# A three-layer perceiver block for 16 pairs of batches: every engine's order of work written anew

## The chip, the cores and the metric

The kernel runs on one core of a Trainium2 chip, in one launch. The metric is the device time of that core in microseconds, a median over runs. Five engines have programs of their own and meet only at semaphores: TensorE (PE, matmuls and transposes), VectorE (DVE), ScalarE (ACT), GpSimd (POOL) and SyncE (SP, which here only issues DMAs).

## The reference

Input are x, 32 batches of 64 rows of 512, and a context of 128 rows of 512 for each batch, all in float32. Three residual layers follow, each on the layer-normalised x:

```python
# 1: cross attention, 16 heads, low-rank
C_q, C_kv = norm(x) @ Wq_d, ctx @ Wkv_d                 # 512 -> 64, 512 -> 32
scores = einsum((C_q @ W_qk) per head, C_kv) / sqrt(32)   # 16 x (64 x 128) a batch
x = x + softmax(scores) @ (C_kv @ Wv_u)
# 2: self attention over the 64 rows, one head of width 128
q, k, v = norm(x) @ Wqkv + bqkv
x = x + softmax(q k^T / sqrt(128)) v @ Wo + bo
# 3: quantised layer
xh = norm(x) @ hadamard                                   # 512 x 512
xq = clip(round(xh / s), -8, 7) * s,  s = max|xh| / 7 of the row
x = x + xq @ ternary(weight)^T
```

## The kernel before

The 32 batches are worked as 16 pairs; a pair's 2 x 64 rows fill the 128 partitions. A pair goes through a chain of small steps, each a matmul group into one PSUM bank and a read of it by ScalarE or VectorE:

- latents: the columns of x and of the context (tiles xt, ct) give the latents (L633, L645; copy to lat), these give q_t (L669) and, spread by a matmul with a folded identity, ckv (L683).
- cross attention: scores of 16 heads into four banks (L612), maxima of eight heads at a time (L435) and their scaling by the row's layer-norm factor (L439), sixteen exponentials on ScalarE (L310 and L313; those of L310 sum their rows too, those of L313 leave the sum to VectorE, L532), a 32 by 32 transpose of the probabilities on VectorE (L445), the weighted sum of the latents into the same four banks (L716, copy u_t), its expansion (L730, tile xo in PSUM), the division by the row sums and the residual (L451, L457: x2).
- self attention: statistics on VectorE (L464), the normalised x2n on GpSimd (L262), its transpose (L638), q, k and v (L655, 24 matmuls into one bank), scores (L678), maximum, exponential (L361), transpose of p (L697), product with v (L706, o2t), output (L722), residual (L556: x3), transpose of x3 (L737).
- quantised layer: the Hadamard product (L622, the costliest group), the row's largest magnitude (L492), rounding by adding a large constant (L340, L508), transpose (L661), the ternary product in bf16 (L691, L701), scaling (L549), residual on GpSimd (L294) and the store.

The order of each engine is written out by hand in a function `body(i, ...)`, one for each engine. Round i holds, on every engine, the latents of pair i+1, the cross attention of pair i, the self attention of pair i-1 and the quantised layer of pair i-2. An engine takes its instructions strictly in that order; what it waits for are the counters `made`, `read` and `done`, through `after`. Rounds -1 to 3 and 12 to 17 are written out, rounds 4 to 11 are a hardware loop of two rounds a turn:

```python
with eng.Fori(*LOOP) as j:
    body(j * 2, j, 0, True, True, True, True)
    body(j * 2 + 1, j, 1, True, True, True, True)
```

PSUM has eight banks: 0 to 3 hold the scores and then the weighted sums, so scores(i+1) wait for the copy of u of pair i. The four others (B1 to B4) are shared: B1 by q, k, v and ckv and xo, B2 by the transposes and q_t, B3 by the latents and the small products of the self attention, B4 by the quantised layer. One-off work lies in the first rounds: the centred query weights, the constant row of the biases, the ternary weights (VectorE, L412 to L427, then transposed by L597), the Hadamard matrix less its row mean (GpSimd, L283 to L289).

## Time and profile before

| | |
|---|---|
| median of 3 runs | 357.31 us (356.91 to 358.39) |
| the profiled execution: its time, its span | 358.43 us, 356.6 us |
| TensorE busy | 308.3 us, 86% of the span, 4612 matmuls |
| VectorE busy | 251.1 us, 70% |
| ScalarE busy | 191.7 us, 54% |
| GpSimd busy | 93.1 us, 26% |
| chain that ended last | PE 35%, DVE 25%, ACT 24%, issue 11% |
| read from memory, written | 20.71 MB, 4.19 MB |

The span is the time from the first to the last instruction. A busy share is the mean over stages that are not alike, and the ends of matmuls are modelled: whether TensorE is at its limit in a stage is read from the starts of its groups. A chain's shares tell who held the end back, each for a part of the time.

### The profile page before, as it was taken

How to read it: one execution, taken by the hardware profiler on the slowest of the kernel's cores; microseconds unless marked ns; L12 is line 12 of the kernel's file. 1: busy time of each engine (PE TensorE's matmuls, PEld its weight loads, DVE VectorE, ACT ScalarE, POOL GpSimd, SP SyncE). 2: the span in 40 equal slices, each digit the busy share in tenths (PEclk: the TensorE clock that was granted, in tenths of full speed). 3: DMA queues.
4: the chain of work that ended last, by engine and by line, in shares of the span. 5: the costliest groups of instructions: out<-in, count | busy, mean ns of one | idle time of the engine just before them, and what ended most of it. 6: DMA issues, size and time to landing. Idle time of an engine off the chain costs nothing.

```text
span 356.6 us, 11424 instructions
## 1 busy us (share of the span) xinstructions
PE 308.3 (86%) x4612; PEld 203.9 (57%) x4612; DVE 251.1 (70%) x530; ACT 191.7 (54%) x629; POOL 93.1 (26%) x133
## 2 busy tenths in 40 slices
PE   5766759999798999899999999999999999968871
PEld 3445447665456566666666565657575666645520
DVE  1454883878587787778787878788787878767432
ACT  1360652847547483829384756657484839282210
POOL 2004232323212221314132323222222223131321
PEclk9995687999999999999999999999999999998997
DMA  7980210303113130303040312213132020000000
GB/s 219 332 304 2 67 54 8 113 4 93 56 35 119 33 118 31 118 29 118 3 141 3 102 45 51 96 29 118 31 119 63 2 61 2 33 2 31 0 31 29
DMA packets 13345, 25.37 MB, mean 71 GB/s; under 512 B 3200, under 2 KB 3712, under 8 KB 13312
## 3 DMA queue, kind: packets, MB, share of 16 engines
q1 hardware_dynamic: 13312, 24.91, 21.5%
q8 instruction: 23, 0.38, 0.4%
q14 instruction: 10, 0.08, 0.1%
HBM read 20.71 MB, written 4.19 MB: 70 GB/s over the span
## 4 chain that ended last, share of the span: by engine, by line
PE 35%; DVE 25%; ACT 24%; issue 11%; POOL 2%; DMA 1%; POOLq 0%; DVEq 0%; ACTq 0%
ACT prob L313 11%; DVE mx L435 10%; PE ps L716 9%; PE ps L612 6%; PE ps L722 5%; PE ps L730 4%; DVE nmx L439 3%; ACT prob L310 3%; PE ps L737 3%; DVE stat L464 3%; DVE stat L483 3%; PE ps L706 2%; POOL rstd L267 2%; ACT q_t L301 2%; ACT p2t L301 2%
## 5 line engine op out<-in xcount | busy, mean ns | idle before, releaser
L310 ACT ACTIVATE prob<-ps,nmx,qk_scale 128x128 f32<-128x128 f32 x128 | 56.7, 457 | 39.5 <-DVE nmx L439 39.5
L622 PE MATMUL ps<-had_s,x3t 128*128 128x512 f32 x128 | 59.2, 606 | 1.4 <-ACT x3t L301 1.4
L313 ACT ACTIVATE prob<-ps,nmx,qk_scale 128x128 f32<-128x128 f32 x128 | 48.5, 489 | 0.0
L435 DVE TENSOR_REDUCE mx<-ps 128x8 f32<-128x1024 f32 x32 | 39.0, 1220 | 10.0 <-PE ps L612 10.0
L445 DVE STREAM_TRANSPOSE prob_t<-prob 128x1024 f32<-128x1024 f32 x32 | 39.1, 1223 | 6.9 <-ACT prob L313 6.9
L294 POOL TENSOR_TENSOR res<-prod,x 128x512 f32<-128x512 f32 x16 | 20.2, 1264 | 82.0 <-DVE prod L549 82.0
L622 PEld LDWEIGHTS ps<-had_s,x3t 128*128 128x128 f32 x128 | 23.0, 190 | 27.2 <-issue 25.3
L655 PEld LDWEIGHTS ps<-x2t,wqkv_s 128*128 128x128 f32 x256 | 30.9, 198 | 10.4 <-ACT x2t L301 10.4
L716 PE MATMUL ps<-prob_t,ckv_n 32*32 32x128 f32 x2048 | 33.1, 300 | 4.0 <-DVE prob_t L445 2.5
L655 PE MATMUL ps<-x2t,wqkv_s 128*128 128x128 f32 x256 | 33.9, 288 | 2.9 <-ACT x2t L301 1.4
L259 POOL TENSOR_TENSOR rstd<-aux,power 128x1 f32<-128x1 f32 x16 | 8.8, 548 | 91.5 <-DVE aux L470 91.5
L716 PEld LDWEIGHTS ps<-prob_t,ckv_n 32*32 32x32 f32 x2048 | 26.2, 108 | 8.4 <-issue 4.9
L556 DVE SCALAR_TENSOR_TENSOR x<-ps,rsum,x2b 128x512 f32<-128x512 f32 x16 | 12.0, 751 | 26.7 <-PE ps L722 26.7
L301 ACT ACTIVATE x3t<-ps 128x512 f32<-128x512 f32 x16 | 9.6, 597 | 33.9 <-PE ps L737 33.9
L310 ACT ACTIVATION_READ_ACCUMULATOR prob<-ps,nmx,qk_scale 128x1 f32 x128 | 26.1, 204 | 0.0
L301 ACT ACTIVATE u_t<-ps 128x512 f32<-128x512 f32 x16 | 9.6, 597 | 30.6 <-PE ps L716 30.6
L279 POOL TENSOR_TENSOR qk_scale<-aux,power 128x1 f32<-128x1 f32 x16 | 8.8, 548 | 61.5 <-DVE aux L518 61.5
L669 PE MATMUL ps<-lat,wqk 128*128 128x128 f32 x128 | 19.7, 302 | 4.3 <-ACT lat L301 4.3
L730 PEld LDWEIGHTS ps<-wv_bd,u_t 128*128 128x128 f32 x128 | 17.0, 201 | 9.2 <-issue 8.7
L612 PE MATMUL ps<-ckv,q_t 32*64 32x128 f32 x1024 | 20.9, 296 | 0.6 <-ACT ckv L301 0.6
L669 PEld LDWEIGHTS ps<-lat,wqk 128*128 128x128 f32 x128 | 17.2, 209 | 6.0 <-ACT lat L301 6.0
L276 POOL TENSOR_TENSOR x2b<-x,const_row 128x512 f32<-128x512 f32 x16 | 20.4, 1274 | 0.0
(112 smaller groups left out, 559.7 us busy)
## 6 DMA issues: line engine op xcount, KB each, us to landing
ct<-ctx_cols SPq DMA_DIRECT2D x16, 512.0 KB, 4.0
xt<-x_cols SPq DMA_DIRECT2D x16, 256.0 KB, 2.7
xr<-x_rows SPq DMA_DIRECT2D x16, 256.0 KB, 2.7
y<-res SPq DMA_DIRECT2D x16, 256.0 KB, 3.6
w_rows<-weight SPq DMA_DIRECT2D x1, 1024.0 KB, 7.9
had_s<-hadamard SPq DMA_DIRECT2D x1, 1024.0 KB, 7.0
wqkv_s<-wqkv SPq DMA_DIRECT2D x1, 768.0 KB, 8.3
wqk<-w_qk SPq DMA_DIRECT2D x2, 128.0 KB, 4.5
```

What stands on the lines that cost most here:

```text
L276: nc.gpsimd.tensor_tensor(x2b[:], x2[:], const_row[:], ALU.add).then_inc(done["x2b"], 1)
L301: return nc.scalar.activation(dst, src, ACT.Copy)
L310: last = nc.scalar.activation(prob[:, h, :], score, ACT.Exp, bias=nmx[:, h:h + 1], scale=scale, accum_out=sum_a[:, h:h + 1])
L313: last = nc.scalar.activation(prob[:, h, :], score, ACT.Exp, bias=nmx[:, h:h + 1], scale=scale)
L435: V.tensor_reduce(mx[:, h], ps[:, 2 * half:2 * half + 2, :].rearrange("p r (c k) -> p (r c) k", c=EC), AX.X, ALU.max).then_inc(done["mx"], 1)
L445: return V.transpose(prob_t[:, 2 * half:2 * half + 2, :, :, :].rearrange("p r c b q -> p (r c b q)"), prob[:, 8 * half:8 * half + 8, :].re ...
L612: mm = pe.matmul(ps[64 * bb:64 * bb + 64, r, c * P:(c + 1) * P], q_t[g, bb, c, :], ckv[g, par, bb * SKV:(bb + 1) * SKV], start=True, stop= ...
L622: mm = pe.matmul(ps[:, B4, :], x3t[:, c, :], had_s[:, c, :], start=(c == 0), stop=(c == EC - 1))
L655: mm = pe.matmul(ps[:, B1, s * P:(s + 1) * P], w if s < 2 else xc, xc if s < 2 else w, start=(c == 0), stop=(c == EC - 1))
L669: mm = pe.matmul(ps[:, B2, c * P:(c + 1) * P], wqk2[:, c * P:(c + 1) * P], lat[:, 0:P], start=True, stop=True)
L716: mm = pe.matmul(ps[32 * r:32 * r + 32, b, 0:P].rearrange("p (c q) -> p c q", c=EC), ckv_n[g, b // 2, kb, :], prob_t[g, r, :, kb, :], star ...
L730: mm = pe.matmul(ps[:, B1, c * P:(c + 1) * P], u_t[:, c, :], wv_bd[:, c, :], start=True, stop=True)
```

## The change

The two-round `body` and the loop go; each step becomes a small function of the pair's number, and each engine gets a list of calls: one list ahead of round 4, one `rnd(i)` that Python repeats for rounds 4 to 11 (all written out in the program), and one list behind. Each function still waits for its own data and buffers.

In a middle round, the latents' matmuls are now those of pair i+2 and their reads q_t and ckv those of i+1 and i+2 as the lists say; xo, the residual and the q, k projection are those of pair i-1, the rest of the self attention and the Hadamard product those of pair i-2, the ternary product that of pair i-3. v is a group of its own. Names in the new lists for TensorE: cq, ckvp are L633, L645; qt is L669; foldkv L683; scores L612; weighted L716; xo L730; x2T L638; qk and val the 16 and the 8 matmuls of L655; s2 L678; p2T L697; o2 L706; out2 L722; x3T L737; had L622; qiT L661; ternary L691 and L701.

Banks are dealt anew: latents and the transpose of p in B4; q_t, ckv, xo, the transpose of x2n and q, k in B3; the small products, the output, the transpose of x3 and the Hadamard product in B2; v and the quantised products in B1. q_t and the third layer's factor get two buffers. A second pair of tiles, xs, holds the rows of x for the statistics of the first layer; so each pair's rows are loaded twice, and the residual's load (xr) comes later. The row sums that VectorE makes are those of the first eight heads, those that ScalarE's exponentials make are of the last eight. The one-off work is cut into pieces: the ternary weights in four, and they and the constants stand in other places.

```diff
-LOOP = (2, 6)
+FIRST, LAST = 4, 12
...
+        xs = sb("xs", [P, 2, E])
...
+        q_t = sb("q_t", [P, 2, 2, EC, SQ])
...
-        qit_bank = ps[:, B4, :].bitcast(BF16)[:, 0:E]
+        qit_bank = ps[:, B1, :].bitcast(BF16)[:, 0:E]
...
+            def load_stat_rows(n):
+                after(sp, done["stat1"], n - 2)
+                sp.dma_start(xs[:, n % 2], x_rows[bass.ds(n, 1)].rearrange("o p e -> (o p) e")).then_inc(ld_xs[n % 2], 16)
...
+            load_cols(2)
+            load_rows(0)
+            load_stat_rows(2)
...
+            load_cols(3)
+            load_rows(1)
+            load_stat_rows(3)
+            load_cols(4)
+            load_rows(2)
+            load_cols(5)
+            load_stat_rows(4)
+            load_rows(3)
+            load_cols(6)
+            load_stat_rows(5)
+            store(0)
+            load_rows(4)
+            load_cols(7)
+            load_stat_rows(6)
+
+            def rnd(i):
+                load_rows(i + 1)
+                load_cols(i + 4)
+                load_stat_rows(i + 3)
+                store(i - 3)
+
+            for i in range(FIRST, LAST):
+                rnd(i)
...
+            qks(0); qks(1); hadamard_sum(); rst2(0); norm2(0); centred(0); centred(1); centred(2); centred(3); qks(2)
+            bias2(0); rst3(0); qks(3); rst2(1); flo3(0); norm2(1); qks(4); bias2(1); bias2(2); rst2(2); norm2(2)
+            rst3(1); flo3(1); qks(5); result(0)
+
+            def rnd(i):
+                rst2(i - 1); norm2(i - 1); result(i - 3); rst3(i - 2); flo3(i - 2); bias2(i - 1); qks(i + 2)
+
+            for i in range(FIRST, LAST):
+                rnd(i)
+            bias2(11); rst2(11); norm2(11); rst3(10); flo3(10); result(9); rst2(12); norm2(12); bias2(12); qks(14)
+            rst3(11); flo3(11); result(10); rst3(12); flo3(12); rst2(13); norm2(13); qks(15); bias2(13); result(11)
+            rst2(14); norm2(14); bias2(14); rst3(13); flo3(13); result(12); rst2(15); norm2(15); rst3(14); flo3(14)
+            bias2(15); result(13); result(14); rst3(15); flo3(15); result(15)
...
+                    if h >= 8:
+                        last = nc.scalar.activation(prob[:, h, :], score, ACT.Exp, bias=nmx[:, h:h + 1], scale=scale,
+                                                    accum_out=sum_a[:, h:h + 1])
...
+            latc(0); ckc(0); qtc(0); latc(1); exps(0, 0, 6); ckc(1); exps(0, 6, 8); exps(0, 8, 16); latc(2)
+            scale_copy(); qtc(1); utc(0); ckc(2); exps(1, 0, 6); hadamard_mean(); qtc(2); exps(1, 6, 8)
+            exps(1, 8, 10); x2tc(0); exps(1, 10, 16); ternary_copy(0); latc(3); vc(0); qkc(0); utc(1); exp2(0)
+            p2tc(0); ckc(3); o2tc(0); exps(2, 0, 8); exps(2, 8, 10); x3tc(0); exps(2, 10, 16); qtc(3); x2tc(1)
+            latc(4); quant(0); ternary_copy(1); utc(2); qkc(1); exp2(1); ckc(4); vc(1); p2tc(1); exps(3, 0, 2)
+            o2tc(1); exps(3, 2, 8); exps(3, 8, 10); x3tc(1); exps(3, 10, 16); qtc(4); latc(5); x2tc(2); utc(3)
+            quant(1); qkc(2); exp2(2); ckc(5); vc(2); p2tc(2)
+
+            def rnd(i):
+                exps(i, 0, 2); o2tc(i - 2); exps(i, 2, 8); exps(i, 8, 10); x3tc(i - 2); exps(i, 10, 16)
+                qtc(i + 1); x2tc(i - 1); latc(i + 2); utc(i); quant(i - 2); qkc(i - 1); exp2(i - 1); ckc(i + 2)
+                vc(i - 1); p2tc(i - 1)
+
+            for i in range(FIRST, LAST):
+                rnd(i)
+            exps(12, 0, 2); o2tc(10); exps(12, 2, 8); exps(12, 8, 10); x3tc(10); exps(12, 10, 16); qtc(13); latc(14)
...
+            ckvT(0); st1(0); wabs(); largest(0, 0); wscale(); largest(0, 1); ternary(0); sums(0); turned(0, 0)
+            turned(0, 1); wide_v_bias(); st1(1); ternary(1); rsums(0); ternary(2); largest(1, 0); xmul(0); xadd(0)
+            st2(0); largest(1, 1); ternary(3); turned(1, 0); st1(2); const(); ckvT(1); turned(1, 1); st1(3); sums(1)
+            max2(0); rsums(1); ckvT(2); largest(2, 0); rsum_2(0); largest(2, 1); xmul(1); x3_(0); xadd(1); st3(0)
+            st2(1); turned(2, 0); turned(2, 1); absmax(0); step(0); sums(2); ints(0); rsums(2); ckvT(3); st1(4)
+            max2(1); largest(3, 0); largest(3, 1); xmul(2); qscales(0); rsum_2(1); x3_(1); intsT(0); xadd(2)
+            turned(3, 0); st2(2); st3(1); turned(3, 1); product(0); absmax(1); step(1); sums(3); qscales(1); rsums(3)
+            st1(5); ints(1); max2(2)
+
+            def rnd(i):
+                largest(i, 0); largest(i, 1); rsum_2(i - 2); xmul(i - 1); x3_(i - 2); intsT(i - 3); xadd(i - 1)
+                ckvT(i); st2(i - 1); turned(i, 0); product(i - 3); turned(i, 1); st3(i - 2); absmax(i - 2)
+                st1(i + 2); step(i - 2); sums(i); ints(i - 2); qscales(i - 2); rsums(i); max2(i - 1)
+
+            for i in range(FIRST, LAST):
+                rnd(i)
+            largest(12, 0); rsum_2(10); largest(12, 1); xmul(11); x3_(10); ckvT(12); intsT(9); xadd(11); turned(12, 0)
+            st2(11); product(9); turned(12, 1); st3(10); absmax(10); sums(12); step(10); ckvT(13); st1(14); rsums(12)
...
+            def qt(n):
+                if n == 0:
+                    pe.wait_ge(ld_w["wqk"], 32)
+                after(pe, read["lat"], n)
+                if edge(n, 2):
+                    after(pe, read["ckv"], n)
+                else:
+                    after(pe, done["xm"], n - 2)
...
+            def foldkv(n):
+                if n == 0:
+                    pe.wait_ge(fold_made, 2)
+                after(pe, read["lat"], n)
+                if edge(n, 3):
+                    after(pe, read["qt"], n - 1)
+                else:
+                    after(pe, read["qk"], n - 3)
+                pe.matmul(ps[:, B3, 0:2 * SKV], fold4[:].rearrange("p r l -> p (r l)"), lat[:, P:P + 2 * SKV],
+                          start=True, stop=True).then_inc(made["ckv"], 1)
...
+            def xo(n):
+                if n == 0:
+                    pe.wait_ge(ld_w["wv"], 64)
+                after(pe, read["u"], n)
+                if edge(n, 0, PAIRS - 2):
+                    after(pe, read["qk"], n - 1)
+                else:
+                    after(pe, read["ckv"], n + 2)
...
+            def val(n):
+                if n == 0:
+                    pe.wait_ge(ld_w["wqkv"], 16)
+                    pe.wait_ge(const_ready, 1)
+                if n == 1:
+                    pe.wait_ge(ternt_read, 2)
+                after(pe, read["x2t"], n)
+                after(pe, read["int"], n - 2)
+                for c in range(EC):
+                    mm = pe.matmul(ps[:, B1, 0:P], x2t[:, c, :], wqkv_s[:, c, 2 * P:3 * P], start=(c == 0),
+                                   stop=(c == EC - 1))
+                mm.then_inc(made["v"], 1)
...
+            def s2(n):
+                if n == 0:
+                    pe.wait_ge(ternt_read, 1)
+                after(pe, read["had"], n - 1)
+                after(pe, read["qk"], n)
+                for bb in range(2):
+                    h = slice(64 * bb, 64 * bb + 64)
+                    mm = pe.matmul(ps[h, B2, 0:SQ], q2[:, h], k2[:, h], start=True, stop=True)
+                mm.then_inc(made["s2"], 1)
...
+            cq(0); ckvp(0); foldkv(0); qt(0); scores(0); cq(1); ckvp(1); cq(2); foldkv(1); qt(1); wide_scale()
+            ckvp(2); weighted(0); foldkv(2); scores(1); xo(0); cq(3); hadamard_mean(); qt(2); wide_bias(); ckvp(3)
+            x2T(0); qk(0); ternary_turned(0); val(0); weighted(1); s2(0); foldkv(3); scores(2); p2T(0)
+            ternary_turned(1); o2(0); xo(1); out2(0); cq(4); ckvp(4); x3T(0); qt(3); had(0); x2T(1); weighted(2)
+            qk(1); scores(3); s2(1); foldkv(4); val(1); p2T(1); xo(2); o2(1); cq(5); out2(1); qiT(0); qt(4); x3T(1)
+            ternary(0); ckvp(5); had(1); x2T(2); weighted(3); qk(2)
+
+            def rnd(i):
+                scores(i); s2(i - 2); foldkv(i + 1); val(i - 2); p2T(i - 2); xo(i - 1); o2(i - 2); cq(i + 2)
+                out2(i - 2); qiT(i - 3); qt(i + 1); x3T(i - 2); ckvp(i + 2); ternary(i - 3); had(i - 2); x2T(i - 1)
+                weighted(i); qk(i - 1)
+
+            for i in range(FIRST, LAST):
+                rnd(i)
+            scores(12); s2(10); foldkv(13); val(10); p2T(10); xo(11); o2(10); cq(14); out2(10); qiT(9); qt(13)
+            x3T(10); ckvp(14); ternary(9); had(10); x2T(11); weighted(12); qk(11); scores(13); s2(11); foldkv(14)
+            val(11); p2T(11); xo(12); o2(11); cq(15); out2(11); qt(14); x3T(11); qiT(10); ckvp(15); had(11); x2T(12)
+            ternary(10); qk(12); weighted(13); s2(12); foldkv(15); scores(14); p2T(12); val(12); xo(13); o2(12)
+            qiT(11); out2(12); qt(15); x3T(12); ternary(11); had(12); x2T(13); weighted(14); qk(13); scores(15)
+            s2(13); xo(14); val(13); p2T(13); qiT(12); o2(13); out2(13); ternary(12); x3T(13); x2T(14); had(13)
+            qk(14); weighted(15); s2(14); val(14); xo(15); p2T(14); qiT(13); o2(14); out2(14); x3T(14); x2T(15)
+            had(14); qk(15); ternary(13); s2(15); val(15); p2T(15); o2(15); qiT(14); out2(15); ternary(14); x3T(15)
+            had(15); qiT(15); ternary(15)
 
```

## Rows read from the trace of the kernel before

**Rows 1.** Chain of work that ended last: start us, us, what.

```profile
34.44 2.02 PE ps L612 x64
...
60.43 1.15 PE ps L612 x63
...
99.89 1.15 PE ps L612 x63
...
138.06 1.21 PE ps L612 x61
...
157.28 1.15 PE ps L612 x63
...
176.02 1.19 PE ps L612 x60
...
251.90 1.15 PE ps L612 x62
...
308.35 1.15 PE ps L612 x63
```

**Rows 2.** Windows: stretch, length, then busy us of each engine, granted clock, DMA.

```profile
35.30:60.40 25.10, 19.23 (x273) 13.70 (x261) 17.08 (x30) 12.95 (x40) 8.01 (x8) 0.74 0.14 44
157.20:176.00 18.80, 17.98 (x288) 11.92 (x287) 15.03 (x33) 11.64 (x39) 5.16 (x7) 1.00 0.21 70
```

**Rows 3.** Timeline of TensorE's matmuls in one looped round: start, us, group.

```profile
157.21 1.21 PE L612 MATMUL ps<-ckv,q_t 32*64 32x128 f32 x64
158.34 3.70 PE L622 MATMUL ps<-had_s,x3t 128*128 128x512 f32 x8
161.97 0.66 PE L633 MATMUL ps<-xt,wq_c 128*64 128x128 f32 x8
...
164.04 2.05 PE L655 MATMUL ps<-x2t,wqkv_s 128*128 128x128 f32 x16
...
168.43 0.34 PE L678 MATMUL ps<-k,q 128*64 128x64 f32 x4
...
169.24 0.60 PE L691 MATMUL ps<-tern_t,qi_t 128*128 128x512 bf16 x2
170.08 0.33 PE L697 MATMUL ps<-ident,p 64*64 64x64 f32 x4 [0.25 <-ACT p L361]
170.34 0.60 PE L701 MATMUL ps<-tern_t,qi_t 128*128 128x512 bf16 x2
171.11 0.46 PE L706 MATMUL ps<-p2t,v 128*128 128x128 f32 x2 [0.17 <-ACT p2t L301]
171.50 1.90 PE L716 MATMUL ps<-prob_t,ckv_n 32*32 32x128 f32 x128
173.33 1.13 PE L722 MATMUL ps<-wo_s,o2t 128*128 128x512 f32 x2
174.29 1.05 PE L730 MATMUL ps<-wv_bd,u_t 128*128 128x128 f32 x8
175.40 0.63 PE L737 MATMUL ps<-ident,x 128*128 128x128 f32 x4
176.00 0.37 PE L612 MATMUL ps<-ckv,q_t 32*64 32x128 f32 x8
```

**Rows 4.** Chain of work, then timeline, of the first round.

```profile
15.61 3.62 ACT prob L310 x16
...
17.09 2.28 DVE L412 TENSOR_REDUCE w_abs<-w_rows 128x4 f32<-128x2048 f32 x1
...
19.47 2.93 ACT L313 ACTIVATE prob<-ps,nmx,qk_scale 128x128 f32<-128x128 f32 x8
...
28.86 2.81 PE L716 MATMUL ps<-prob_t,ckv_n 32*32 32x128 f32 x128 [2.55 <-DVE prob_t L445]
```

**Rows 5.** Timeline of TensorE just ahead of the loop.

```profile
96.82 0.44 PE L716 MATMUL ps<-prob_t,ckv_n 32*32 32x128 f32 x13 [1.47 <-issue]
```

**Rows 6.** The page: bytes moved by DMA in each of 40 slices.

```profile
GB/s 219 332 304 2 67 54 8 113 4 93 56 35 119 33 118 31 118 29 118 3 141 3 102 45 51 96 29 118 31 119 63 2 61 2 33 2 31 0 31 29
```

More of the change, by code:

```diff
@@ L141, in perceiver_kernel @@
         ld_ct = [sem(f"ld_ct{i}") for i in range(2)]
+        ld_xs = [sem(f"ld_xs{i}") for i in range(2)]
         ld_xr = [sem(f"ld_xr{i}") for i in range(2)]
@@ L232, in _ @@
-            looped(sp, body)
-            store(PAIRS - 1, (PAIRS - 1) % 2)
-            for par in range(2):
-                sp.wait_ge(res_free[par], 16 * (1 + PAIRS // 2))
+            load_cols(3)
[10 more added lines that the diff above has]
+            load_rows(4)
@@ new lines, in _ @@
+            load_cols(7)
[7 more added lines that the diff above has]
+                rnd(i)
+            load_rows(13)
+            load_stat_rows(15)
+            store(9)
+            load_rows(14)
+            store(10)
+            load_rows(15)
+            for n in range(11, PAIRS):
+                store(n)
@@ L740, in _, with edge, cq @@
-            looped(pe, body)
+            def edge(n, lo, hi=PAIRS):
+                return not lo <= n < hi
+            def cq(n):
+                loaded(pe, ld_xt, n)
+                if edge(n, 4):
+                    after(pe, read["lat"], n - 1)
+                else:
+                    after(pe, read["p2t"], n - 4)
+                for h in range(2):
+                    for t in range(2):
+                        c = 2 * t + h
+                        pe.matmul(ps[64 * t:64 * t + 64, B4, 0:P], wq_c[:, c, :], xt[:, n % 2, c, :],
+                                  start=(h == 0), stop=(h == 1))
@@ new lines, in o2, with out2, x3T @@
+            def o2(n):
+                after(pe, read["v"], n)
+                after(pe, read["p2t"], n)
+                pe.matmul(ps[:, B2, 0:P], v2[:], p2t[:], start=True, stop=True).then_inc(made["o2t"], 1)
+            def out2(n):
+                after(pe, read["o2t"], n)
+                pe.matmul(ps[:, B2, :], o2t[:], wo_s[:], start=True, stop=True).then_inc(made["wo"], 1)
+            def x3T(n):
+                after(pe, read["wo"], n)
+                for c in range(EC):
+                    mm = pe.transpose(ps[:, B2, c * P:(c + 1) * P], x3[:, n % 2, c * P:(c + 1) * P], ident[:])
+                mm.then_inc(made["x3t"], 1)
@@ new lines, in had, with qiT @@
+            def had(n):
+                if n == 0:
+                    pe.wait_ge(had_ready, EC)
+                after(pe, read["x3t"], n)
+                for c in range(EC):
+                    mm = pe.matmul(ps[:, B2, :], x3t[:, c, :], had_s[:, c, :], start=(c == 0), stop=(c == EC - 1))
+                mm.then_inc(made["had"], 1)
+            def qiT(n):
+                if edge(n, 0, PAIRS - 1):
+                    after(pe, read["int"], n - 1)
+                else:
+                    after(pe, read["v"], n + 1)
+                after(pe, done["qi"], n)
+                for c in range(EC):
+                    mm = pe.transpose(qit_bank[:, c * P:(c + 1) * P], qi[:, c * P:(c + 1) * P], ident_b[:])
+                mm.then_inc(made["qit"], 1)
```

859 lines of the change are left out of this document (392 added, 467 removed).

## The prediction

> **What bounds the kernel now.** I read the chain of work first, for the start of each round, since a round begins where the matmuls of L612 appear in it [rows 1]. Rounds 4 to 11 last 152.0 us, 19.0 each (99.89 to 251.90); before them stand 99.9 us for four rounds, after them 56.5 for three, and 48.3 from the last scores to the end. In the looped rounds 19.2 (138.06 to 157.28) and 18.7 (157.28 to 176.02) take turns: the turn of the loop costs 0.5 every second round. Then the table by stretches [rows 2]: in one round of 18.8 us TensorE is busy 17.98, VectorE 15.03, ScalarE 11.64, GpSimd 5.16. So TensorE is near its limit in the middle. How near, its own timeline of that round tells [rows 3], start to start, because ends are modelled and overlap. The round lasts 18.79 us (157.21 to 176.00). In it TensorE came late in these places. Between the first pair of ternary matmuls and the transpose of p, 0.84 us stand for two matmuls that need 0.43 (two in 0.6 us less the overlap seen between neighbours): 0.41. Between the second pair and the next, 0.77 for the same: 0.34. Before L737, 1.11 us for eight matmuls which in the 24 of L655 take 0.118 each: 0.16. Before L730, 0.96 for two of 0.43: 0.10. From 161.97 to 164.04, 2.07 for three groups that I put at 1.80: 0.27. From 164.04 to 168.43, 4.39 for work that I put at 4.17: 0.22. Together 1.5 us, so **the matrix work of a round is 17.3 us**. The rest of the 19.0 is waiting and the loop.
>
> At the ends TensorE is far from its limit: at 60.43 only round 2 starts, and the granted clock in the stretch up to there is 0.74 [rows 2], that is, a good part of it at 1.2 of 2.4 GHz. The matmuls of L716 took 2.81 us there [rows 4], against 1.83 from start to start in the middle [rows 3].
>
> **The change part by part.** No arithmetic is removed. TensorE's 24 projection matmuls become 16 (q, k) and 8 (v); the reads by ScalarE and VectorE keep their count, and the row sums of eight heads stay on VectorE, only of the other half. New are a second load of each pair's rows (16 times 256 KB) and a loop written out.
>
> *The middle rounds.* I traced the new order of one round, from T, the start of scores(i), with durations of the middle rounds. TensorE: scores to 1.13, s2 1.40, fold 1.94, v 2.9, transpose of p, xo 4.1, o2 4.4, cq 5.0, out2 5.9, qiT 6.1, qt 7.2, x3T 7.8, ckv 8.4, ternary 9.3, Hadamard 12.9, x2T 13.5, weighted 15.3, q and k 17.2. What each waits for: p's exponential needs s2, two small VectorE steps and ScalarE, and is there at about 2.6, with p's transpose due at 2.9. ScalarE then copies latents, v and p, and begins the sixteen exponentials at 3.9, later than now, when nothing stands ahead of them. They cost 3.6 and 2.9 us for eight each [rows 4] and hold two copies (0.9), so they end at 11.2; VectorE turns the second half until 12.8; weighted is due at 13.5. The copy of u ends at 16.1, the next scores come at 17.2. q and k are read until 0.9 after them, s2 is due at 1.13. x3 needs out2 (5.9), and is written at 6.9, its transpose due at 7.2. VectorE has 15.8 us of work by its start-to-start sums (busy 15.03 and its small gaps), and in my trace it ends 0.5 before it is needed. So nothing makes TensorE late, and the ring through the exponentials (15.2 us: 3.9, 7.3, 1.6, 1.9, 0.5) is shorter than its own work. The margins are thin, 0.2 to 0.7 in five places, so I take **17.4 us** for a round; ends 17.2 and 19.0. Eight rounds: 139.2 against 152.0, **12.8 us less**. The 0.5 of the loop's turn lies in this.
>
> A round written out is fetched in a straight line. The trace shows one stall in the middle of the matmuls of weighted, 1.47 us with nothing that it waited for [rows 5], just ahead of the loop, in some ten rounds of straight code. Eight more such rounds: 0 to 1.5 us, I take 0.4; a stall in each round would be 1.5 times 8. The Trainium skill, page Runtime: NRT & Kernel Launch, section Instruction fetch mechanics, says that straight code is fetched ahead without a stall and that a taken branch out of the window causes one; by it the 0.4 would be nothing. The trace agrees on the branch (19.2 against 18.7) and not wholly on the straight code.
>
> The added rows cost 4.2 MB. Early on the queues move 332 GB/s in a slice [rows 6]; four of the loads fall in it, 1.0 MB, 3 us of transfer that push the late weights from about 25 to 28 us; q, k of pair 0 need them after 44. Nothing. The other twelve lie where the slices show 2 to 141 GB/s. On SyncE each round's row load waits for x2, its columns for the latents two rounds ahead, the store for the result; all are freed by 8 us of my round except the store (13), behind which no load stands that is needed within the round.
>
> *The start.* Round 0 gets slower: fold now stands ahead of qt in one bank, 0.8 us, and the reduction of the weights, 2.28 us [rows 4], ahead of the first maximum, 1.8; copies stand between the exponentials. They end at 26 instead of 22.4. But the constants no longer stand between them and the turning: weighted(0) at 27.4 for 28.86 [rows 4]. scores(1) now stand ahead of xo: 31.3 for 34.4 [rows 1]. The quantised weights come in four pieces, three before they bite: weighted(1) at 49. scores(2) stand ahead of out2, xo and x3T: 52.7 for 60.4. Rounds 2 and 3, with 16.5 and 17.9 us (the Hadamard of pair 0 is late there for want of its latents' copies), give scores(4) at 87.1 for 99.9: **12.8 us less**. Bounds: 83 if the clock is full earlier, 95 if the interleaved copies cost what they save.
>
> *Rounds 12 to 14.* 17.4, 17.4 and 16.2 (no new latents): 51.0, with 0.5 for the changed order 51.5, against 56.5: **5.0 less**.
>
> *From the last scores to the end.* The second attention now lags by one more: some 35 us of matrix work are left where before some 30 were, in a chain for pair 15 that I sum to 42.5 us without any other work. Other pairs' Hadamard and ternary matmuls stand in it for 5: 47.5. I take **no gain** (48.3); bounds 45 and 52.
>
> Sum: 12.8 + 12.8 + 5.0 + 0 - 0.4 = 30.2 us. The profiled execution took 358.43 with a span of 356.6; it would take 328.2. The median of the runs shown, 357.31, lies 1.1 below it: **327.1 us**. The measurement can tell about 0.5% from no change.
>
> **The rivals.**
> *Handoffs make the round.* The waits of the new order meet at ScalarE: it must pass s2, exp, two copies before the exponentials. If VectorE is late for the small maximum by 1 us (it has 15.8 us of work and 0.5 of margin), everything behind comes 0.8 later each round: 18.2, over 11 rounds 9 us, 336. For it: VectorE is the second fullest, and its order has four places where it waits in turn for TensorE. Against: in my trace ScalarE, not VectorE, sets the exponentials' start.
> *The start gives nothing.* VectorE's single items (some 13 us) are still in the first rounds; if they only move, 8 of the 12.8 are lost: 335. Against: in [rows 4] weighted(0) waits 2.55 for VectorE only because of the constants.
> *Slower than before: the code is not fetched in time.* One mechanism: all five engines now run straight code, and TensorE's stall of 1.47 us [rows 5] comes again at every stretch of new code. It must come about 21 times, twice a round in rounds 4 to 14, to eat 30.2; at two and a half a round (27) the time is 367. For it: the one stall. Against: the four rounds behind the loop are straight already and show 18.8 us each, without one (a stall would make 20.3).
> *Hardly a change.* The margins of the middle all miss and each round costs 19.0 again: 12.8 and 4.4 of the gain go, 344, still faster; only with the start's gain gone as well is it 355 to 358.
>
> **How the numbers follow.** Forecast 0.62 (its own range 321 to 334), handoffs 0.22 (334 to 344), the start 0.09 (333 to 340), hardly a change 0.03, slower 0.04. The range of 8 in 10 takes the ends of the terms: 17.2 us a round (2.2 less), start 3 less, together 321; above, the handoffs at 18.5 a round: 340. Faster by over 0.5%: 0.93; within: 0.03; slower: 0.04.
>
> **What would show it.** Starts of the scores 17.2 to 17.6 us apart from round 4 on; TensorE busy all of a round; scores(4) at 87; the exponentials beginning 3.9 after the scores and weighted not waiting; no idle time of 1 us put down to issue in the matmuls; 47 to 48 us behind the last scores. I am wrong if the rounds take 18.2 or more, with TensorE waiting for ScalarE's copy of p or VectorE's x3, or if scores(4) come after 95.

## The result, and the profile after

The changed kernel takes 329.68 us (327.18 to 331.48, 4 runs), the kernel before on the same chip 357.85 (356.91 to 360.15, 4 runs): a ratio of 0.9199 [0.9121, 0.9277]. The forecast was 327.1, with a range of 320 to 340. The profiled execution took 330.3 us with a span of 328.4, so 28.2 us less than the 356.6 of before.

The page first: busy time, bytes moved in each slice, and the chain by engine.

```profile
PE 296.2 (90%) x4597; PEld 206.5 (63%) x4612; DVE 246.2 (75%) x530; ACT 197.5 (60%) x629; POOL 94.1 (29%) x133
...
GB/s 221 327 377 161 100 132 4 157 6 0 75 250 69 115 83 81 117 36 160 30 166 11 186 2 195 6 194 2 66 34 34 37 32 36 2 35 0 33 32 32
...
PE 76%; ACT 6%; issue 5%; DVE 4%; SPq 4%; DMA 2%; POOL 1%; POOLq 0%; ACTq 0%; DVEq 0%
```

TensorE's busy time fell from 308.3 to 296.2 us though it does the same matmuls; ends are modelled, and more of the start now runs at the full clock. The windows of 20 to 40 us show it, first before, then after (stretch, length, busy us of PE, PEld, DVE, ACT, POOL, granted clock, DMA share, GB/s):

```profile
20.00:40.00 20.00, 14.65 (x230) 9.98 (x229) 10.41 (x19) 6.18 (x20) 4.69 (x4) 0.74 0.33 117
```

```profile
20.00:40.00 20.00, 15.00 (x254) 10.74 (x254) 14.02 (x22) 9.54 (x31) 4.67 (x3) 0.97 0.52 184
```

TensorE's share of the span rose from 86% to 90%. What tells more is the chain: 76% of what ended last is TensorE's own work, before it was 35%. ScalarE and VectorE, 24% and 25% of the chain before, are down to 6% and 4%. The loads have the same burst at the start and then more in the middle (once 250 GB/s in a slice and then up to 195, before up to 141, [rows 6]).

The starts of the scores in the chain of waits, where [rows 1] had those of before (L779 is the old L612; columns start us, us, what):

```profile
53.13 0.91 PE ps L779 x45
...
86.08 1.14 PE ps L779 x61
...
171.31 1.14 PE ps L779 x62
...
188.27 1.14 PE ps L779 x62
...
274.92 1.14 PE ps L779 x63
```

| stage | before, us | after, us | saved | forecast |
|---|---|---|---|---|
| start, to the scores of pair 4 | 99.89 | 86.08 | 13.8 | 12.8 |
| rounds 4 to 11 | 152.0 | 136.8 | 15.2 | 12.8 (less 0.4 for fetch stalls) |
| rounds 12 to 14 | 56.45 | 52.0 | 4.4 | 5.0 |
| from the last scores to the end | 48.25 | 53.5 | -5.2 | 0 |
| sum | 356.6 | 328.4 | 28.2 | 30.2 |

A regular round now lasts 16.97 us. Here are the windows of such a round and of the end; the round answers to the second line of [rows 2]:

```profile
171.30:188.30 17.00, 16.84 (x294) 12.15 (x301) 14.73 (x35) 12.19 (x39) 5.14 (x7) 1.00 0.26 95
274.90:328.40 53.50, 39.46 (x374) 23.88 (x376) 27.23 (x64) 18.05 (x57) 12.49 (x16) 0.91 0.06 21
```

In the round TensorE is busy 16.84 of 17.00 us; before it was 17.98 of 18.80. The timeline of TensorE in that round, where [rows 3] had the old one (start, us, group):

```profile
171.24 1.21 PE L779 MATMUL ps<-ckv,q_t 32*64 32x128 f32 x64
172.37 0.34 PE L845 MATMUL ps<-k,q 128*64 128x64 f32 x4
...
173.17 1.05 PE L834 MATMUL ps<-wqkv_s,x2t 128*128 128x128 f32 x8
...
174.42 1.16 PE L804 MATMUL ps<-wv_bd,u_t 128*128 128x128 f32 x8
...
179.78 0.81 PE L896 MATMUL ps<-tern_t,qi_t 128*128 128x512 bf16 x3 [0.16 <-issue]
180.43 3.60 PE L880 MATMUL ps<-had_s,x3t 128*128 128x512 f32 x8
183.86 0.60 PE L812 MATMUL ps<-ident,x2n 128*128 128x128 f32 x4
184.39 1.90 PE L790 MATMUL ps<-prob_t,ckv_n 32*32 32x128 f32 x128
186.22 2.05 PE L821 MATMUL ps<-x2t,wqkv_s 128*128 128x128 f32 x16
188.20 0.56 PE L779 MATMUL ps<-ckv,q_t 32*64 32x128 f32 x20
```

Each group begins where the one before ends. There is no wait for another engine in it; the 0.16 put down to issue ahead of the ternary matmuls is the only idle time. Other engines wait for TensorE now: ScalarE's timeline shows the first exponential at 175.07, 3.83 us after the scores (the forecast had 3.9), and a copy that had to wait 1.68 us for TensorE:

```profile
175.07 0.81 ACT L378 ACTIVATE prob<-ps,nmx,qk_scale 128x128 f32<-128x128 f32 x2
...
184.56 0.60 ACT L343 ACTIVATE x2t<-ps 128x512 f32<-128x512 f32 x1 [1.68 <-PE ps L812]
```

### The profile page after: what moved, and what is told of

The parts are those of the page before. It is cut to its first block, busy times and chain, and to the rows that moved or that the text cites. A ratio compares the mean times of both kernels' runs of the same rounds, so it can differ in the third digit from the quotient of the medians.

```text
span 328.4 us, 11515 instructions
## 1 busy us (share of the span) xinstructions
PE 296.2 (90%) x4597; PEld 206.5 (63%) x4612; DVE 246.2 (75%) x530; ACT 197.5 (60%) x629; POOL 94.1 (29%) x133
## 4 chain that ended last, share of the span: by engine, by line
PE 76%; ACT 6%; issue 5%; DVE 4%; SPq 4%; DMA 2%; POOL 1%; POOLq 0%; ACTq 0%; DVEq 0%
PE ps L880 15%; PE ps L821 10%; PE ps L790 8%; PE ps L779 5%; PE ps L867 5%; PE ps L834 5%; PE ps L804 4%; PE ps L896 3%; PE ps L756 3%; PE ps L768 3%; ACT prob L375 2%; DMA xt<-x_cols 2%; PE ps L812 2%; PE ps L735 2%; PE ps L743 2%
## 5 line engine op out<-in xcount | busy, mean ns | idle before, releaser
L880 PEld LDWEIGHTS ps<-had_s,x3t 128*128 128x128 f32 x128 | 24.1, 193 | 27.8 <-issue 24.1
L821 PE MATMUL ps<-x2t,wqkv_s 128*128 128x128 f32 x256 | 35.0, 291 | 2.2 <-issue 1.2
L821 PEld LDWEIGHTS ps<-x2t,wqkv_s 128*128 128x128 f32 x256 | 31.7, 200 | 7.0 <-issue 5.5
L790 PE MATMUL ps<-prob_t,ckv_n 32*32 32x128 f32 x2048 | 30.4, 278 | 1.5 <-DVE prob_t L548 1.5
L375 ACT ACTIVATION_READ_ACCUMULATOR prob<-ps,nmx,qk_scale 128x1 f32 x128 | 29.0, 226 | 0.0
L790 PEld LDWEIGHTS ps<-prob_t,ckv_n 32*32 32x32 f32 x2048 | 24.6, 103 | 6.3 <-issue 4.4
L554 DVE TENSOR_REDUCE sum_a<-prob 128x8 f32<-128x1024 f32 x16 | 19.5, 1217 | 4.2 <-ACT prob L378 4.2
L343 ACT ACTIVATE x2t<-ps 128x512 f32<-128x512 f32 x16 | 9.6, 598 | 20.8 <-PE ps L812 20.8
L779 PE MATMUL ps<-ckv,q_t 32*64 32x128 f32 x1024 | 21.0, 288 | 1.1 <-ACT q_t L343 0.7
L756 PEld LDWEIGHTS ps<-lat,wqk 128*128 128x128 f32 x128 | 17.6, 212 | 5.8 <-issue 5.7
L436 ACT ACTIVATE z<-ps,round_c,qinv 128x512 f32<-128x512 f32 x16 | 12.4, 778 | 12.7 <-DVE qinv L626 12.6
L779 PEld LDWEIGHTS ps<-ckv,q_t 32*64 32x64 f32 x1024 | 16.4, 135 | 4.5 <-issue 1.9
```

The costliest lines, as they stand in the source:

```text
L375: last = nc.scalar.activation(prob[:, h, :], score, ACT.Exp, bias=nmx[:, h:h + 1], scale=scale, accum_out=sum_a[:, h:h + 1])
L554: V.tensor_reduce(sum_a[:, 0:8], prob[:, 0:8, :], AX.X, ALU.add).then_inc(done["sum"], 1)
L756: mm = pe.matmul(ps[:, B3, c * P:(c + 1) * P], wqk2[:, c * P:(c + 1) * P], lat[:, 0:P], start=True, stop=True)
L779: mm = pe.matmul(ps[64 * bb:64 * bb + 64, r, c * P:(c + 1) * P], q_t[g, n % 2, bb, c, :], ckv[g, n % 2, bb * SKV:(bb + 1) * SKV], start=Tr ...
L790: mm = pe.matmul(ps[32 * r:32 * r + 32, b, 0:P].rearrange("p (c q) -> p c q", c=EC), ckv_n[g, b // 2, kb, :], prob_t[g, r, :, kb, :], star ...
L821: mm = pe.matmul(ps[:, B3, s * P:(s + 1) * P], wqkv_s[:, c, s * P:(s + 1) * P], x2t[:, c, :], start=(c == 0), stop=(c == EC - 1))
```

## The experiments

The kernel before ran beside each; every ratio is to it. All windows of rounds named below are at a granted clock of 1.00 unless said.

### The loop alone written out (b_unroll)

```diff
             at = pipeline(body)
-            with eng.Fori(*LOOP) as j:
-                body(j * 2, j, 0, True, True, True, True)
-                body(j * 2 + 1, j, 1, True, True, True, True)
-            for i in range(2 * LOOP[1], PAIRS + 2):
+            for i in range(2 * LOOP[0], PAIRS + 2):
                 at(i)
```

> The kernel before with its loop written out and nothing else changed. Theory (the new order filled TensorE's waits): only the four turns of the loop go, 0.4 to 0.5 us each, so 1.6 to 2.0 us less, about 355.5 us; rounds 4 to 11 take 18.8 us each. Rival (the loop was the cost): most of the 28 us goes, 335 us or less. Rival (straight code is fetched too late): stalls in matmul groups put down to issue, 360 us or more.

360.07 us (358.16 to 363.81), ratio 1.0048 [1.0014, 1.0083]: a miss, no gain but rather a loss, and close to the 360 of the reading in which stalls appear. The regular rounds are 18.82 us each, so the 0.4 of the loop's turn is gone as expected. What came in its place stands in TensorE's timeline, two of three such gaps inside the matmuls of weighted (the third is 0.91 at 96.32):

```profile
173.19 0.47 PE L713 MATMUL ps<-prob_t,ckv_n 32*32 32x128 f32 x21 [1.25 <-issue]
...
306.77 0.41 PE L713 MATMUL ps<-prob_t,ckv_n 32*32 32x128 f32 x3 [1.38 <-issue]
307.11 1.70 PE L719 MATMUL ps<-wo_s,o2t 128*128 128x512 f32 x2
```

The one at 96.32 stands where the kernel before has its own of 1.47 [rows 5]; the two others are new, 2.6 us together. Behind the last, L719 takes 1.70 us for the 1.13 of its twin L722 in [rows 3], and the granted clock of 306 to 312 is 0.72: this round lasted 22.0, 3.2 more than its neighbours. The round with the gap of 1.25 lasted 20.36, 1.5 more than its neighbours. So 1.5 and 3.2 are lost, and 1.4 (eight rounds by 0.18) and 0.5 (scores of pair 4 at 99.38 for 99.89) won: 2.8 more, of the 3.0 by which the two profiled spans differ; the medians of that chip differ by 1.3. So the loop written out is no source of the gain.

The trace has a hint of what these gaps are. The profile lists the transfers of an instruction queue, 16 KB each, first for the kernel before, then for b_unroll (number, MB, share of 16 engines):

```profile
q8 instruction: 23, 0.38, 0.4%
```

```profile
q8 instruction: 36, 0.59, 0.7%
```

In b_unroll one of them lands 0.3, 0.1 and 0.0 us ahead of the three gaps (they start at 94.1, 170.6 and 304.0), and in the kernel before one lands right ahead of the gap of 1.47. Many others, as the one at 182.7, have no such gap behind them, so this fits late instructions but does not prove them.

### v apart alone (b_vapart)

The kernel before with v as its own eight matmuls behind s2, foldkv behind the product with v, and the copies of both moved with them.

```diff
-                    for s in range(3):
+                    for s in range(2):
...
+                if self_:
+                    for c in range(EC):
+                        mm = pe.matmul(ps[:, B1, 2 * P:3 * P], x2t[:, c, :], wqkv_s[:, c, 2 * P:3 * P],
+                                       start=(c == 0), stop=(c == EC - 1))
+                    mm.then_inc(made["v"], 1)
```

> The kernel before, loop kept, with v taken out of the group of 24 matmuls: 8 matmuls behind the small scores s2, foldkv moved behind the product with v, and ScalarE's copies of v and ckv moved with them. Theory: q and k are ready 0.95 us earlier, and the v matmuls stand where TensorE waited for p (0.41 and 0.34 us a round), so a round takes 18.2 to 18.4 us instead of 19.0 and the kernel 346 to 350 us. Rival (each round is set by the ring through the exponentials): the scores-to-scores time stays at 18.7 to 19.2 and the kernel at 355 to 359.

371.21 us (370.36 to 372.21), ratio 1.0377 [1.0320, 1.0434]: a clear miss, the wrong way. Rounds last 19.65 and 20.08 in turn. TensorE's timeline of one:

```profile
161.94 1.21 PE L615 MATMUL ps<-ckv,q_t 32*64 32x128 f32 x64
...
171.91 0.40 PE L663 MATMUL ps<-ident_b,qi 128*128 128x128 bf16 x4 [1.07 <-DVE qi L511]
...
173.18 0.34 PE L680 MATMUL ps<-k,q 128*64 128x64 f32 x4
...
175.36 0.33 PE L696 MATMUL ps<-ident,p 64*64 64x64 f32 x4 [0.32 <-ACT p L364]
...
177.14 1.90 PE L723 MATMUL ps<-prob_t,ckv_n 32*32 32x128 f32 x128
...
181.64 0.62 PE L615 MATMUL ps<-ckv,q_t 32*64 32x128 f32 x25
```

TensorE reached the transpose of the rounded rows (L663) earlier, by the v that had stood ahead of it, and waited 1.07 us there for VectorE. s2 began 11.24 us after the scores, as before (11.22 in [rows 3]); the v matmuls then stood behind it and pushed weighted to 15.20 after the scores, from 14.29. The moved work filled no gap: it opened one upstream and lengthened the path downstream. In the changed kernel v is apart too, no wait stands around it (173.17), and there the rounded rows that L663 waited for belong to a pair one round older. That this lag is what makes the cut harmless I read from the two orders; no run changed the lag alone.

### One more matmul in each round (b_peplus, a_peplus)

```diff
                     after(pe, read["x3t"], n)
+                    pe.matmul(ps[:, B2, :], x3t[:, 0, :], had_s[:, 0, :], start=True, stop=True)
                     for c in range(EC):
```

(In the kernel before the same ahead of its L622, in bank B4.)

> The kernel before with one float32 matmul of 128x512 more for each pair, in front of the Hadamard group, its result overwritten (0.86 us of TensorE at full clock). Theory (TensorE has 1.5 us of waits a round, part of them behind this group): some is absorbed, 0.4 to 0.8 us more a round, in all 7 to 12 us. If TensorE is not the limit at all: under 3 us.

> The changed kernel with one float32 matmul of 128x512 more for each pair, in front of the Hadamard group, its result overwritten (0.86 us of TensorE at full clock). Theory (TensorE has no wait left in the middle rounds): rounds of 16.97 become 17.83, all of it is paid in rounds 2 to 15, 13 to 15 us in all. Rival (handoffs set the round): under 0.4 us a round, under 6 us in all.

Chains of waits, first the kernel before with it, then the changed one:

```profile
161.00 1.14 PE ps L612 x62
...
180.41 1.18 PE ps L612 x58
```

```profile
177.87 1.14 PE ps L779 x63
...
195.70 1.20 PE ps L779 x61
```

Before: 19.42 us a round for a mean of 19.0, so 0.4 of the 0.86 is paid and the rest falls into waits. In the written-out rounds behind the loop it is more, 19.40 for 18.82, so 0.6 of 0.86 is paid there: the waits that work in this place can fill are 0.3 to 0.4 us, not all of the 1.5. The whole took 369.6, but its two runs, 366.85 and 372.35, lie 5.5 us apart; both are within the 7 to 12 us more that was expected. The profile is of the longer one, whose end stands at a granted clock of 0.86; the rounds shown stand at 1.00. After: 17.83 = 16.97 + 0.86, the whole price in each round, and 340.87 in all (339.71 to 342.02, 2 runs), ratio 0.9527 [0.9445, 0.9608]. That is 11.4 us more than the next two kernels, run on the same chip, which time as the changed kernel does; less than the 13 to 15 expected. 16 times 0.86 is 13.8. The two profiled spans differ by 9.5: 2.7 up to the scores of pair 4, 5.9 in rounds 4 to 11 (8 times 17.83, without the two long rounds that cost the changed kernel 1.1), 1.3 in rounds 12 to 14, and 0.3 less at the end. So what is missing falls into waits behind round 11. The changed kernel's middle is bound by TensorE; the old one's was not, quite.

### A shorter sum on VectorE (b_shortsum, a_shortsum)

```diff
-                    V.tensor_reduce(sum_a[:, 8:16], prob[:, 8:16, :], AX.X, ALU.add).then_inc(done["sum"], 1)
+                    V.tensor_reduce(sum_a[:, 8:16], prob[:, 8:16, 0:16], AX.X, ALU.add).then_inc(done["sum"], 1)
```

(In the changed kernel the same for heads 0 to 7. Both leave out 112 of the 128 elements of each of these sums.)

> The kernel before with the row sums of eight heads taken over 16 of their 128 elements, which takes about 1.0 us of VectorE from each round (the sums are then not those of the reference). Theory (TensorE's waits, not VectorE's load): the sum stands behind the last transpose that TensorE waits for, so 0 to 2 us less in all. Rival (VectorE sets the round): 0.8 us a round, 12 us less.

> The changed kernel with the row sums of eight heads taken over 16 of their 128 elements, about 1.0 us of VectorE less in each round (the sums are then not those of the reference). Theory: no change in the middle, rounds stay at 16.97; 0 to 2 us less at the ends. Rival (VectorE is the limit now): rounds of 16.2 to 16.5, 6 to 10 us less.

358.19 us, ratio 0.9988 [0.9957, 1.0018], rounds 18.75 and 19.2 as they were; and 329.26 (327.57 to 330.95), ratio 0.9203 [0.9114, 0.9291], rounds 16.97 (157.14 to 174.11 in its chain). VectorE's load limits the middle of neither kernel, though it was the second fullest and in the forecast the main rival's cause. Its steps that others wait for, as the maxima, were not made shorter in either.

### The rows loaded once (a_onerow)

The changed kernel with one tile of four buffers for both readers of x's rows: 4.2 MB less.

```diff
-        xs = sb("xs", [P, 2, E])
-        xr = sb("xr", [P, 2, E])
+        xr = sb("xr", [P, 4, E])
...
-            def load_rows(n):
-                after(sp, read["xo"], n - 2)
-                sp.dma_start(xr[:, n % 2], x_rows[bass.ds(n, 1)].rearrange("o p e -> (o p) e")).then_inc(ld_xr[n % 2], 16)
+                after(sp, read["xo"], n - 4)
+                sp.dma_start(xr[:, n % 4], x_rows[bass.ds(n, 1)].rearrange("o p e -> (o p) e")).then_inc(ld_xr[n % 4], 16)
```

> The changed kernel without the second load of the rows: one tile of four buffers serves both the statistics and the residual (4.2 MB less from memory), all orders kept. Theory (the queues are not what anything waits for in the middle, and early they are): rounds unchanged; the start gains up to 1 us because less stands ahead of the columns of pair 2; 327 to 330 us. Rival (the added transfers cost): 3 us or more less.

329.48 us (328.80 to 330.24), ratio 0.9202 [0.9147, 0.9257], beside 0.9199 for the changed kernel. The second load costs nothing that can be measured, and brings nothing by itself. Nor did the start gain the up to 1 us hoped for: the scores of pair 4 come at 87.28.

### The changed kernel again, and its start (after_again, a_cols)

> The changed kernel as it is, on the same chip as the three kernels run with it: 327 to 331 us.

329.04 us (327.49 to 331.96, 6 runs), ratio 0.9205 [0.9165, 0.9246]. In its profile the end took 51.5 us (span 324.8). The start in the changed kernel's own trace had shown TensorE waiting for the columns of pair 2 (timeline of TensorE):

```profile
21.17 1.12 PE L735 MATMUL ps<-xt,wq_c 128*64 128x128 f32 x8 [3.99 <-DMA xt<-x_cols]
...
29.51 1.89 PE L790 MATMUL ps<-prob_t,ckv_n 32*32 32x128 f32 x128 [0.84 <-DVE prob_t L548]
...
32.18 1.20 PE L779 MATMUL ps<-ckv,q_t 32*64 32x128 f32 x64
```

They were queued behind the Hadamard matrix (1 MB) and four small weight loads. a_cols moves them ahead:

```diff
             sp.dma_start(wo_s[:], wo).then_inc(ld_w["wo"], 16)
+            load_cols(2)
             sp.dma_start(had_s[:], hadamard.rearrange("(c p) n -> p c n", p=P)).then_inc(ld_w["had"], 16)
...
-            load_cols(2)
             load_rows(0)
```

> The changed kernel with the columns of pair 2 issued ahead of the Hadamard matrix and the four small weight loads. In the changed kernel's trace TensorE waits 4.0 us for them (15.1 to 21.2) and the chain of waits goes through this load. Theory (this load holds the start back): latents of pair 2 at 17 to 18, weighted(0) 2 to 3.5 us earlier, scores(4) at 83 to 84.5, 2 to 3 us less in all. Rival (VectorE's one-off work or the Hadamard's row mean is next): under 1 us less, or slower if the Hadamard matrix comes later than 28 us.

324.96 us (323.04 to 327.13, 6 runs), ratio 0.9069 [0.9030, 0.9107]: 4.1 us less than after_again on the same chip, more than the 2 to 3 expected.

```profile
18.41 0.66 PE L735 MATMUL ps<-xt,wq_c 128*64 128x128 f32 x8 [0.83 <-DMA xt<-x_cols]
...
26.23 2.37 PE L790 MATMUL ps<-prob_t,ckv_n 32*32 32x128 f32 x128 [2.90 <-DVE prob_t L548]
...
29.68 1.60 PE L779 MATMUL ps<-ckv,q_t 32*64 32x128 f32 x64
```

The wait shrank from 3.99 to 0.83, weighted(0) begins at 26.23 instead of 29.51, the scores of pair 4 at 82.53 instead of 86.08 (85.65 in after_again). So 3.1 to 3.6 us of the 4.1 are seen at this stage. What ends last at weighted(0) is now the turning of the probabilities on VectorE, for which it waits 2.90.

### Two tries at the end (a_tail, a_both, a_best)

In the changed kernel's end whole groups of pair 14 stand in the chain of pair 15. Timeline of TensorE:

```profile
298.11 1.12 PE L872 MATMUL ps<-ident,x 128*128 128x128 f32 x4 [0.84 <-DVE x L603]
...
299.97 4.44 PE L880 MATMUL ps<-had_s,x3t 128*128 128x512 f32 x8
304.25 1.95 PE L821 MATMUL ps<-x2t,wqkv_s 128*128 128x128 f32 x16
...
308.00 1.13 PE L834 MATMUL ps<-wqkv_s,x2t 128*128 128x128 f32 x8 [0.55 <-DVE prod L650]
...
310.25 0.46 PE L863 MATMUL ps<-p2t,v 128*128 128x128 f32 x2 [0.87 <-ACT p2t L343]
...
314.51 3.70 PE L880 MATMUL ps<-had_s,x3t 128*128 128x512 f32 x8 [0.75 <-ACT x3t L343]
```

a_tail puts the Hadamard product of pair 14 into a bank that the scores have left, in four pieces between the steps of pair 15, and moves the reads with it:

```diff
-            had(14); qk(15); ternary(13); s2(15); val(15); p2T(15); o2(15); qiT(14); out2(15); ternary(14); x3T(15)
-            had(15); qiT(15); ternary(15)
+            had14(0); qk(15); had14(1); s2(15); ternary(13); val(15); p2T(15); had14(2); o2(15); had14(3); out2(15)
+            x3T(15); qiT(14); had(15); ternary(14); qiT(15); ternary(15)
```

> The changed kernel with the end reordered: the Hadamard product of pair 14 in a free score bank, in four pieces between the steps of pair 15, and the reads that go with it moved. Theory (the end is a chain of pair 15 into which whole groups of pair 14 are put): q and k of pair 15 start 3 us earlier, the time behind the last scores falls from 53.5 to 49.5 to 51 us, 2.5 to 4 us less in all. Rival (the chain waits for VectorE or for the clock at half rate in any case): under 1 us less.

329.82 us (326.21 to 330.86, 6 runs), ratio 0.9184 [0.9139, 0.9229] beside after_again's 0.9205 [0.9165, 0.9246]: a miss, no gain. Its timeline, all engines:

```profile
305.36 1.13 PE L834 MATMUL ps<-wqkv_s,x2t 128*128 128x128 f32 x8 [1.05 <-DVE prod L650]
...
318.11 1.26 POOL L324 TENSOR_TENSOR res<-prod,x 128x512 f32<-128x512 f32 x1 [4.25 <-DVE prod L650]
318.30 1.36 DVE L631 TENSOR_SCALAR qi<-z 128x512 bf16<-128x512 f32 x1 [0.27 <-ACT z L436]
```

q and k of pair 15 began 4.0 us earlier (300.27 for 304.25) and the last Hadamard product 2.1 earlier (312.45 for 314.51). But part of that is the clock of the changed kernel's profile. Beside after_again, counted from the last scores, q and k are 2.6 earlier, the last Hadamard product is 0.7 earlier, and the end is 1.1 longer (52.6 for 51.5). Two waits are longer: v(15) waits 1.05 for VectorE's product of pair 13, for 0.55, and at 318.30 VectorE's rounding takes 1.36 us, for 0.43 where nothing runs beside it, while GpSimd's residual of pair 14 (318.11) runs. With both edits (a_both):

> Both edits, of the start and of the end. Theory: they add up, 4.5 to 7 us less than the changed kernel, 322 to 325 us.

326.13 us (325.71 to 326.97, 6 runs), ratio 0.9097 [0.9068, 0.9125]: a miss (322 to 325 were expected), not better than a_cols alone, and both waits are there again (1.05 and the rounding of 1.36). In this profile the last Hadamard product also takes 5.40 us for the 3.70 of a_tail, in an end at a granted clock of 0.91. a_best is a_both with both waits taken away: v(15) goes to a free bank, the ternary product of pair 13 ahead of s2(15), VectorE's product of pair 13 ahead of the row sum, and GpSimd holds its residual of pair 14 until pair 15 is rounded.

```diff
+                if n == PAIRS - 2:
+                    after(pool, done["qi"], PAIRS - 1)
...
-            max2(15); rsum_2(15); product(13); absmax(14); step(14); x3_(15); qscales(14); ints(14); st3(15); intsT(14)
+            max2(15); product(13); rsum_2(15); absmax(14); step(14); x3_(15); qscales(14); ints(14); st3(15); intsT(14)
...
-            had14(0); qk(15); had14(1); s2(15); ternary(13); val(15); p2T(15); had14(2); o2(15); had14(3); out2(15)
+            had14(0); qk(15); ternary(13); s2(15); val(15); had14(1); p2T(15); had14(2); o2(15); had14(3); out2(15)
```

> The changed kernel with the earlier columns of pair 2 (measured alone: 4 us less) and a second try at the end. Beside the Hadamard product of pair 14 in four pieces, v of pair 15 now lies in a free score bank, so that it waits for no product of pair 13 (1.05 us lost in the first try), and GpSimd's last but one residual waits until VectorE has rounded pair 15 (in the first try that rounding took 1.36 us beside it, 0.43 alone). Theory (the end is a chain, and these were the two new waits in it): the time behind the last scores is 49.5 to 51 us, scores(4) at 82.5 to 83.5, in all 321 to 324 us, 1 to 3 us under the earlier columns alone. Rival (the spread of the clock at the ends is larger than such edits): within 1.5 us of the earlier columns alone, 323.5 to 326.5.

323.10 us (321.88 to 325.02, 6 runs), ratio 0.9028 [0.8979, 0.9076], the fastest of all here and within the 321 to 324 expected. Behind the last scores stand 49.7 us, at a mean granted clock of 0.95; in a_cols, whose end is the changed kernel's, it is 51.8 at the same 0.95 (a_tail 52.6 at 0.93, a_both 54.0 at 0.91). Its timeline:

```profile
313.41 0.43 DVE L633 TENSOR_SCALAR qi<-z 128x512 bf16<-128x512 f32 x1 [0.27 <-ACT z L438]
...
313.98 1.27 POOL L326 TENSOR_TENSOR res<-prod,x 128x512 f32<-128x512 f32 x1 [5.00 <-DVE prod L652]
```

The rounding is back at 0.43, and the residual runs behind it. So it was the residual beside it that made it long. Against a_cols (0.9069 [0.9030, 0.9107], another chip) the intervals overlap, so the end's part of the gain, about 2 us, is shown by its stage in one profile each and not by the time alone.

## Why the prediction was right

*What bounds the kernel.* Right: the late places in the round of before were waits. The same matmuls now fit in 16.97 us, 1.8 less than the 18.79 of that round, for the 1.5 counted. Work added to TensorE was in part absorbed there and is paid in full now. But no run took the new order apart further than v: what the deeper lag, the new banks and the second buffers each bring is not shown.

*The middle rounds: 17.4 us taken, 16.97 measured.* The mechanism held, point by point: exponentials 3.83 after the scores (3.9), over at 11.1 (11.2), weighted at 13.15 (13.5) with nothing to wait for, s2 right behind the scores. The size was off by 0.4, and the 16.97 lies outside the 17.2 to 17.6 that I had named as the sign, for two reasons. I had put 0.2 on top of the order's 17.2 for thin margins, and none of them was missed; and 17.2 itself was summed from start-to-start times of before that still held small waits, as the 3.63 us of its Hadamard product [rows 3], now 3.43. Two of the eight rounds were longer, 17.37 and 17.67, which leaves 15.2 us saved for 12.8.

*Fetch stalls: 0.4 us taken.* About right in size for the eight rounds meant. The changed kernel shows one in them, in the longer of the two rounds, inside the q and k matmuls:

```profile
205.11 0.83 PE L821 MATMUL ps<-x2t,wqkv_s 128*128 128x128 f32 x6 [0.54 <-issue]
```

Another of 0.67 stands ahead of 274.10, in the same kind of group, so it is 1.2 us in all; b_unroll shows three, 3.5 us. Their place comes with the code: a_cols and a_tail have the first of the two at the same matmul (0.54, 0.55), six other profiles the second (0.39 to 0.67), and four kernels of the old order have theirs ahead of the last 13 matmuls of the same weighted (0.91 to 1.47). Their size, and whether they come at all, changes from one execution to the next: after_again has none of 0.3 us or more in rounds 4 to 11. So the whole kernel pays 1.2 to 3.5 us in these two profiles, and where it falls is known only from a profile. The Trainium skill, page Runtime: NRT & Kernel Launch, section Instruction fetch mechanics, has straight code fetched ahead nearly for free and names the taken branch as the cost. The runs here show the other balance: the turn of the loop cost 0.4 us in two rounds, written out it was replaced by stalls of 1.25 and 1.38. That these stalls are instruction fetch is my reading; the trace says only that the engine waited for nothing it shows, and that a transfer of the instruction queue had landed up to 0.3 us before (0.9 us in the changed kernel). The rival that made them decide needed some 21, and fell.

*The start: 12.8 forecast, 13.8 measured.* The single anchors came 0.4 to 2.1 us late: weighted(0) at 29.51 (27.4), scores(1) 32.18 (31.3), weighted(1) 50.34 (49), scores(2) 53.08 (52.7). I had let the constants go from the path but not looked at what else SyncE's queue put ahead of the columns of pair 2; a_cols shows this at 3.1 to 3.6 us by the scores of pair 4. Rounds 2 and 3 then ran at the new pace, 15.8 and 17.2 us for the 16.5 and 17.9 forecast, and more than made it up. The forecast had the clock only in a bound (83 if it is full earlier); but at 0.97 for 0.74 between 20 and 40 us the same matmuls are shorter, weighted(0) 1.89 us for 2.81. How much of the 13.8 is the clock and how much the moved one-off work, no run separates.

*Rounds 12 to 14:* 4.4 for 5.0, one of the three taking 18.1 us where the order changes, the others 17.0 and 16.9.

*The end: the mis-sized term.* No gain was forecast, with bounds of 45 and 52 us; it takes 53.5, 5.2 more than before and outside them (51.5 in after_again, 3.2 more and just inside). The windows of both ends tell how; this is the one of the kernel before, beside that of the changed kernel's above:

```profile
308.35:356.60 48.25, 32.88 (x337) 19.30 (x336) 24.76 (x59) 15.92 (x49) 11.26 (x15) 0.92 0.05 19
```

TensorE has 39.46 us of work in the new end for 32.88 in the old: 6.6 more, since the second attention and the ternary product lag by one more. I had expected the old end's idle time to take it up. It took 1.4: idle 14.0 for 15.4. The reason is in the timeline of the end: at the last pair every step waits for its predecessor, and the matmuls of pair 14 don't stand in those gaps, they stand in whole groups ahead of pair 15's next step (the Hadamard product at 299.97, 4.44 us ahead of q and k of pair 15, 3.70 at the full clock), while the gaps (0.84, 0.55, 0.87, 0.75) stay open elsewhere. I had put other pairs' matmuls in this chain at 5 us without writing out which gaps could hold them. a_best, which cuts that group in pieces, has 49.7.

Is it the clock? Both ends above have nearly the same, 0.92 and 0.91, so it does not make the 5.2. It moves the end from one execution to the next all the same. The window of 300 to 305 us, first of the changed kernel, then of its second profile:

```profile
300.00:305.00 5.00, 5.00 (x16) 2.70 (x16) 0.55 (x1) 0.60 (x1) 1.64 (x3) 0.85 0.00 0
```

```profile
300.00:305.00 5.00, 4.60 (x28) 2.86 (x26) 1.77 (x5) 1.29 (x3) 0.24 (x1) 1.00 0.00 0
```

The granted clock is 0.85 in the first and 1.00 in the second, whose end took 51.5 in place of 53.5 at a mean of 0.95 for 0.91. The last Hadamard product but one, at 299.97, takes 4.44 us for the 3.70 of the next.

*The added loads:* nothing, as forecast (a_onerow). *The rivals:* the start gave all it was to give, and no round kept its 19.0. Handoffs at 18.2 us a round did not come, and a_shortsum shows that VectorE's load does not set the round: taking 1.0 us from it changed none.

*The sum.* 28.2 us for 30.2, and part of that closeness is luck: the start and the middle gave 3.8 more than forecast, rounds 12 to 14 and the end 5.8 less.

## What to carry to other kernels

Where one engine is busy most of a stage and late in many small places, a new order of all engines can close them together, while a single move of the same set (v apart) cost 3.8%. Add a known amount of work to the suspected engine: if a round grows by half of it, waits are there to fill; if by all of it and the engine's timeline shows no wait, that engine is the limit. The second condition is needed, since work put into a chain of handoffs would be paid in full too. Deeper lag is paid at the end: write out which gap each late group goes into, and count what doesn't fit.
